# W2 of a macaron block halved to f16 and turned by DMA before its last butterfly

## The reference

```
x = x + 0.5 * ffn(layernorm(x), W1, W2, W3)
x = x + attn(layernorm(x), qkv_w, qkv_norm_w, proj_w, proj_norm_w, norm_w, s)
x = x + 0.5 * ffn(layernorm(x), W1, W2, W3)

ffn(x):  hidden = fwht(silu(x @ W1.T) * (x @ W3.T))      # H = 2048, Hadamard transform over H, / sqrt(H)
         return hidden @ W2.T
attn:    q, k, v = rmsnorm(x) @ ternary(qkv_w).T          # weights rounded to -1, 0, 1 times a scale
         16 heads of 32, decaying linear attention in chunks of 128, two rmsnorms, @ ternary(proj_w).T
```

## Time and profile before

| | us |
|---|---|
| median of 3 runs (lowest, highest) | 2405.73 (2405.51, 2408.26) |
| profiled execution: own time | 2411.79 |
| profiled execution: span | 2410.1 |
| TensorE busy | 2366.8 |
| VectorE busy | 1173.1 |
| ScalarE busy | 719.5 |
| GpSimd busy | 162.8 |
| first stage ends | 111.1 |
| second stage ends | 207.6 |
| W2 stage ends | 232.2 |
| first down stage ends | 278.0 |

### The profile page before, as it was taken

The page is one execution under the profiler, slowest core; times in us unless marked ns, Lnnn a source line. Parts: engine busy times, 40 slices in busy tenths (PEclk is TensorE's granted clock), DMA queues, the critical chain, the costliest instruction groups (busy, mean ns, idle before and its releaser), DMA issues.

```text
span 2410.1 us, 32239 instructions
## 1 busy us (share of the span) xinstructions
PE 2366.8 (98%) x13040; PEld 1143.9 (47%) x13040; DVE 1173.1 (49%) x2091; ACT 719.5 (30%) x1205; POOL 162.8 (7%) x111
## 2 busy tenths in 40 slices
PE   7998999999999999999999999999999999999999
PEld 3444445544454455445544554455445544544444
DVE  6566535454455534554455355534564445445312
ACT  6635323222232222232323232232233222222211
POOL 0192000000000000000000000000000000000000
PEclk9999999999999999999999999999999999999999
DMA  7933422042213311222133122301331223020210
GB/s 196 220 134 97 126 88 57 23 133 51 75 40 105 75 45 58 83 66 82 34 114 66 40 79 70 109 27 40 105 75 58 62 53 92 23 79 18 70 35 18
DMA packets 240067, 182.20 MB, mean 76 GB/s; under 512 B 172208, under 2 KB 196784, under 8 KB 236080
## 3 DMA queue, kind: packets, MB, share of 16 engines
q1 hardware_dynamic: 239632, 179.63, 26.9%
q10 hardware_dynamic: 288, 0.52, 0.1%
HBM read 84.68 MB, written 54.53 MB: 58 GB/s over the span
## 4 chain that ended last, share of the span: by engine, by line
PE 91%; DVE 4%; DMA 2%; issue 1%; ACT 1%; SPq 1%; POOL 0%; DVEq 0%; ACTq 0%; POOLq 0%
PE d_bank L1378 26%; PE l_bank L1358 25%; PE g_bank L1358 25%; PE a_bank L1416 5%; PE a_bank L1403 2%; PE a_bank L1482 2%; PE a_bank L1470 2%; PE a_bank L1434 1%; PE a_bank L1464 1%; DVE work L1096 1%; PE a_bank L1448 1%; DVE work L1076 0%; DMA w1t<-q_parts 0%; PE a_bank L1424 0%; DMA parts_dram<-q_parts 0%
## 5 line engine op out<-in xcount | busy, mean ns | idle before, releaser
L1378 PE MATMUL d_bank<-w2t,work 128*128 128x512 f16 x2940 | 674.5, 380 | 0.0
L1076 DVE SCALAR_TENSOR_TENSOR work<-l_bank,l_scale,work 128x512 f32<-128x512 f32 x256 | 191.8, 749 | 548.9 <-PE l_bank L1358 548.8
L1378 PEld LDWEIGHTS d_bank<-w2t,work 128*128 128x128 f16 x2940 | 284.8, 98 | 331.5 <-issue 1.6
L1358 PE MATMUL g_bank<-xt,w1t 128*128 128x512 f16 x1536 | 354.1, 380 | 4.2 <-issue 1.5
L1358 PE MATMUL l_bank<-xt,w3t 128*128 128x512 f16 x1536 | 352.4, 379 | 2.1 <-DVE work L1076 1.3
L815 ACT ACTIVATE work<-g_bank,g_scale 128x512 f32<-128x512 f32 x256 | 175.4, 685 | 575.7 <-PE g_bank L1358 570.0
L1358 PE MATMUL l_bank<-work,w3t 128*128 128x512 f16 x1344 | 308.3, 379 | 0.2 <-DVE work L1076 0.2
L1358 PE MATMUL g_bank<-work,w1t 128*128 128x512 f16 x1344 | 308.3, 379 | 0.0
L834 ACT CAST work<-work 128x512 f16<-128x512 f32 x232 | 143.3, 618 | 520.1 <-DVE work L1076 518.6
L1358 PEld LDWEIGHTS g_bank<-xt,w1t 128*128 128x128 f16 x1536 | 147.7, 98 | 180.4 <-issue 4.8
L1358 PEld LDWEIGHTS l_bank<-xt,w3t 128*128 128x128 f16 x1536 | 147.7, 98 | 171.9 <-issue 1.5
(11 more groups left out here) (198 smaller groups left out, 1749.6 us busy)
## 6 DMA issues: line engine op xcount, KB each, us to landing
work<-parts_dram SPq DMA_DIRECT2D x192, 128.0 KB, 2.7
x_dram<-work SPq DMA_DIRECT2D x16, 1024.0 KB, 3.9
work<-x_dram SPq DMA_DIRECT2D x11, 1024.0 KB, 6.8
parts_dram<-q_parts SPq DMA_DIRECT2D x32, 256.0 KB, 2.0
parts_dram<-k_parts SPq DMA_DIRECT2D x32, 256.0 KB, 2.0
norm_dram<-cent SPq DMA_DIRECT2D x32, 256.0 KB, 2.0
w2t<-in_L_ffn_W_dram SPq DMA_DIRECT2D x30, 256.0 KB, 3.3
xin<-in_L_attn_x_dram SPq DMA_DIRECT2D x7, 1024.0 KB, 8.1
```

What stands on the lines that cost most here:

```text
L1076: nc.vector.scalar_tensor_tensor(out=hfull, in0=l_bank[:], scalar=l_scale[:, j:j + 1], in1=gate, op0=ALU.mult, op1=ALU.mult).then_inc(hful ...
L1358: ins = nc.tensor.matmul(dst[:], wt[:, wp, k, P * j:P * (j + 1)], src[:, xp, k, :], start=(k == 0 and wp == xp), stop=(k == KT - 1 and wp ...
L1378: ins = nc.tensor.matmul(d_bank[t][:], parts[:, hp, P * t:P * (t + 1)], w2t[:, wp, j, :], start=(j == 0 and hp == wp), stop=(j == HT - 1 a ...
```

## The change

Six edits, all in the preparation:

- The Hadamard product takes over one more of the 11 stages: GpSimd does three stages a quarter of W2 (BUTTERFLIES 4 to 3), and w2pair makes the last one by adding and subtracting the products of block i and block i + 8, with a positive and a negated f16 Hadamard matrix.
- W2 is split into two f16 parts in its own layout (w2split, 16 chunks of 128x512, ScalarE and VectorE, 4 buffers) and each chunk's pair of parts is turned by a DMA transpose from SyncE into w2t. w2turn and the fp32 w2had go. w2pair reads w2t, multiplies in f16 into two alternating pairs of banks, and ScalarE and VectorE write the results back over w2t.
- All of W2 is loaded at row blocks 12 to 15 of the first stage; the squares, butterflies, wtop, wfit and splits all lie in the second stage. The first butterfly writes into xt (w2f[0]) and so waits for the last lin of the first stage.
- The norm of batch 2 moves from the second stage to the first down stage (slots 0 to 5). The load of x for it follows the sums of the qkv_w quarters, whose buffer moved to the memory of the mask.
- The signs are turned by 16 DMA transposes from a ring of four buffers; qturn goes from TensorE and ScalarE. SyncE sends the first one after down 7.
- The reload of the qkv and proj rows (wst) is issued right behind the last W2 split.

```diff
-    BUTTERFLIES = HT.bit_length() - 1
+    BUTTERFLIES = HT.bit_length() - 2
+    CHUNKS = 4
+    TERNS = 4
...
+        qst = x_next
+        w2f = [xt_whole[:]] + [w2n[:, t, :] for t in range(KT - 1)]
...
-        had_bank = [g_bank, l_bank]
-        a_bank16 = [b[:].bitcast(F16).rearrange("p (a k t) -> p a k t", a=2, k=KT) for b in a_bank]
+        pair_bank = [a_bank, [g_bank, l_bank]]
...
-                if j >= HT - 2:
-                    steps += [("w2sum", j - (HT - 2)), flies[j - (HT - 2)]]
-            steps += [("begin", 1), ("next_x", 2)]
+            steps += [("begin", 1), ("next_q", 0)]
             own = {}
-            for q in range(2, 2 * KT):
-                add(own, (4, 4, 9, 9, 16, 16)[q - 2] + q % 2, [("w2sum", q)])
-            for i, fly in enumerate(flies[2:]):
+            for q in range(2 * KT):
+                add(own, q, [("w2sum", q)])
+            for i, fly in enumerate(flies):
                 add(own, 2 * i, [fly])
-            for q in range(2 * FOURTHS):
-                add(own, 3 + 2 * q, [("qsum", (q // 2, q % 2))])
-            for i, part in enumerate(norm_steps(("ffn1", 2))):
-                add(own, 18 + 2 * i, part)
-            add(own, 29, [("wtop", 0)])
-            add(own, 31, [("wfit", 0), ("qmean", 0)])
+            add(own, 9, [("wtop", 0)])
+            add(own, 12, [("wfit", 0)])
+            splits = (13, 14, 16, 18) + tuple(range(19, 31))
+            for i, at in enumerate(splits):
+                add(own, at, [("w2split", i)])
+            for q, at in enumerate((2, 4, 6, 8, 10, 11, 15, 17)):
+                add(own, at, [("qsum", (q // 2, q % 2))])
+            add(own, 21, [("qmean", 0), ("next_x", 2)])
...
+            steps += [("w2pair", i) for i in range(HT // 2)]
+            own = {}
+            for i, part in enumerate(norm_steps(("ffn1", 2))):
+                add(own, i, part)
+            add(own, 6, [("decay", 0)])
+            for i in range(8):
+                add(own, 5 + i, [("qscale", i)])
+                add(own, 7 + i, [("qprep", 2 * i), ("qprep", 2 * i + 1)])
+            add(own, 12, [("fit", 0)])
...
-                    if m and c in (12, 13):
-                        load_w2(0, c % 2)
+                    if m and c >= 12:
+                        load_w2(c - 12, 0)
+                        load_w2(c - 12, 1)
...
+                elif step == "w2split":
+                    t, q = divmod(arg, CHUNKS)
+                    sp.wait_ge(w2_lo, arg + 1)
+                    sp.dma_start_transpose(w2t[:, CHUNKS * q:CHUNKS * (q + 1), :, P * t:P * (t + 1)].rearrange("p j a d -> p (j a) d"),
+                                           w2_parts[arg % 4].rearrange("p j a d -> p (j a d)")).then_inc(w2_turned[arg % 4], 16)
+                    if arg == KT * CHUNKS - 1:
+                        for w in range(FOURTHS):
+                            sp.dma_start(wst[:, 4 * w:4 * w + 4, :], quarter(w)).then_inc(wst_loaded[w], 16)
+                elif step == "qprep":
+                    r = arg
+                    sp.wait_ge(q_tern, r + 1)
+                    if r == 0:
+                        sp.wait_ge(d_step, 8)
+                    dst, col = (wqkv, r) if r < QKV_T else (wproj, r - QKV_T)
+                    sp.dma_start_transpose(dst[:, :, P * col:P * (col + 1)], tern[:, r % TERNS, :]).then_inc(q_turned[r % TERNS], 16)
...
-                    src, dst = (w2n[:, t, :], w2p) if st % 2 == 0 else (w2p, w2n[:, t, :])
+                    src, dst = (w2n[:, t, :], w2f[t]) if st % 2 == 0 else (w2f[t], w2n[:, t, :])
...
+                            pool.wait_ge(l_ready, HT)
...
+                elif step == "w2split":
+                    t, q = divmod(arg, CHUNKS)
+                    act.wait_ge(w2_but, t + 1)
+                    act.wait_ge(w2_f, 1)
+                    if arg < 2:
+                        act.wait_ge(w_turned[2 + arg], 16 * 2 * HT // 4)
+                    elif arg < 4:
+                        act.wait_ge(flipped[arg - 2], flips(("ffn1", 1), arg))
                     else:
+                        act.wait_ge(w2_turned[arg % 4], 16 * (arg // 4))
+                    nc.scalar.activation(w2_parts[arg % 4][:, :, 0, :], w2f[t][:, D * q:D * (q + 1)].rearrange("p (j d) -> p j d", d=P), ACT.Copy,
+                                         scale=w2_scale[:]).then_inc(w2_hi, 1)
+                elif step == "w2pair":
+                    act.wait_ge(w2_had, arg + 1)
+                    for half, j in enumerate((arg, arg + HT // 2)):
+                        nc.scalar.activation(w2t[:, j, 0, :], pair_bank[arg % 2][half][:], ACT.Copy, scale=f2[:, j:j + 1]
+                                             ).then_inc(w2_final_hi, 1)
...
+                    nc.vector.tensor_scalar(w2_scale[:], tiny[:, 5:6], PRE_SCALE, None, ALU.mult)
                     link(power(tiny[:, 4:5], top_all[:, 0:1], True))
+                    nc.vector.tensor_scalar(f2[:], f2[:], tiny[:, 4:5], 2.0 / 2.0 ** 6 * W_SCALE * 0.25 / PRE_SCALE,
+                                            ALU.mult, ALU.mult).then_inc(w2_f, 1)
...
+                elif step == "w2split":
+                    t, q = divmod(arg, CHUNKS)
+                    dve.wait_ge(w2_hi, arg + 1)
+                    parts = w2_parts[arg % 4]
+                    nc.vector.scalar_tensor_tensor(out=parts[:, :, 1, :], in0=w2f[t][:, D * q:D * (q + 1)].rearrange("p (j d) -> p j d", d=P),
+                                                   scalar=w2_scale[:], in1=parts[:, :, 0, :], op0=ALU.mult,
+                                                   op1=ALU.subtract).then_inc(w2_lo, 1)
+                elif step == "w2pair":
+                    for half, j in enumerate((arg, arg + HT // 2)):
+                        dve.wait_ge(w2_final_hi, 2 * arg + half + 1)
+                        nc.vector.scalar_tensor_tensor(out=w2t[:, j, 1, :], in0=pair_bank[arg % 2][half][:], scalar=f2[:, j:j + 1],
+                                                       in1=w2t[:, j, 0, :], op0=ALU.mult, op1=ALU.subtract).then_inc(w2_final_lo, 1)
...
+                    r = arg
+                    if r == 0:
+                        for t in (2, 3):
+                            dve.wait_ge(flipped[t % 2], flips(("ffn1", 2), t))
+                    elif r >= TERNS:
+                        dve.wait_ge(q_turned[r % TERNS], 16 * (r // TERNS))
+                    dve.wait_ge(q_scaled, r + 1)
+                    signs, negative = tern[:, r % TERNS, :], tern[:, TERNS + r % 2, :]
+                    link(nc.vector.tensor_scalar(negative, wst[:, r, :], -0.5, None, ALU.is_lt))
+                    nc.vector.scalar_tensor_tensor(out=signs, in0=wst[:, r, :], scalar=0.5, in1=negative, op0=ALU.is_gt,
+                                                   op1=ALU.subtract).then_inc(q_tern, 1)
...
+                elif step == "w2pair":
+                    i, banks = arg, pair_bank[arg % 2]
+                    if i == 0:
+                        pe.wait_ge(dve_const, 2)
+                        for b in range(4):
+                            pe.wait_ge(w2_turned[b], 16 * KT * CHUNKS // 4)
+                    elif i == 1:
+                        pe.wait_ge(gate_ready, 2 * HT)
+                        pe.wait_ge(hfull_ready, 2 * HT)
                     else:
+                        pe.wait_ge(w2_final_lo, 2 * (i - 1))
+                    for second in range(2):
+                        for j, sign in ((i, 0), (i + HT // 2, second)):
+                            for part in range(2):
+                                ins = nc.tensor.matmul(banks[second][:], hadamard[:, sign, :], w2t[:, j, part, :],
+                                                       start=(j == i and part == 0), stop=(j > i and part == 1))
+                    ins.then_inc(w2_had, 1)
```

More of the change, by code:

```diff
@@ L22 @@
 W_SCALE = 2.0 ** 15
+PRE_SCALE = 2.0 ** 14
 QKV_SCALE = 2.0 ** 6
@@ L59, in macaron_kernel @@
         w3t = sb("w3t", [P, 2, KT, H], F16)
-        w2t = sb("w2t", [P, 2, HT, D], F16)
+        w2t = sb("w2t", [P, HT, 2, D], F16)
         wqkv = sb("wqkv", [P, KT, 3 * D], F16)
@@ L368, in first_steps @@
-            own = {1: [("decay", 0)], 4: [("qscale", 0)], 5: [("qprep", 0), ("qscale", 1)]}
-            for r in range(8):
-                own[6 + r] = [("qturn", r)]
-                if r < 6:
-                    own[6 + r] = [("qscale", r + 2)] + own[6 + r]
-                if r < 7:
-                    own[6 + r] += [("qprep", r + 1)]
-            add(own, 9, [("fit", 0)])
+            steps += [("w2pair", i) for i in range(HT // 2)]
+            own = {}
+            for i, part in enumerate(norm_steps(("ffn1", 2))):
+                add(own, i, part)
@@ L531, in _ @@
                     sp.dma_start(hid_dram[arg], spill[arg % 2]).then_inc(hid_stored[arg % 2], 16)
-                elif step == "w2had" and arg == HT - 1:
-                    for j in (HT - 2, HT - 1):
-                        b, fill = filled("w2turn", j)
```

(35 more changed lines are left out.)

92 lines of the change are left out of this document (21 added, 71 removed).

## The result

The changed kernel is slower: 2416.28 us as the median of 6 runs (2412.47 to 2417.35) against 2406.15 of the kernel before on the same chip (2405.09 to 2408.26), a ratio of 1.0038 with a 95% interval of 1.0026 to 1.0049. The forecast was 2399.7, with a range of 2390 to 2412. The profiled execution after took 2415.66 us, its span is 2413.7.

A forecast was written before the change was run, and what follows sets the result against it. TensorE, busy 98% of the span, was taken as the bound, with only the first 278 us edited. Terms +2.3 - 1.7 - 4.5 - 2.1 = -6.0 us took 2405.7 to 2399.7 us, range 2390 to 2412.

The forecast's parts named there:

- Second stage: Gate and lin of the second feed-forward: fewer butterflies, added splits, 94.8 against 96.5 us, -1.7 (-8 to +7).
- The holds: Second stage: GpSimd's butterflies hold VectorE's splits and low halves, two or three a pair; TensorE stands 9.9 us with wfit.
- First stage: First feed-forward's gate and lin: W2 loads ahead of transposes make the last three gates late, +2.3 us (0 to +6).
- the loads pile up: First stage: three more megabytes push the transposes by 6 instead of 2.3 us, with a restart; +5, 2404.7 us; chance 0.09.
- W2 stage: f16 products replace fp32 transposes and products; with a 3.0 us transpose wait and 1 restart, 20.1 against 24.6: -4.5 us.
- First down stage: Sign transposes leave TensorE, but the residual and next down stage come 1 to 3 us late: -2.1 us (-4.4 to +2).
- The rival of SyncE's ring: First down stage: sign transposes cost 2 us of SyncE's queue each, stage ends 14 us late, 2411.7 us; chance 0.12.
- Sum: Whole kernel: the four stage terms, +2.3 - 1.7 - 4.5 - 2.1, make -6.0 us.
- a sign of being wrong that the prediction had named: Behind the prologue: the prediction is wrong if that unedited part moves by itself.
- The forecast of -6: Whole kernel: -6.0 us from the runs' median of 2405.7, to 2399.7 us.

The follow-up runs named there:

- best_top_elem: best with the maximum reduction behind wtop replaced by an elementwise addition (computes something else): 2396.97 us, ratio 0.9957 to the kernel before.
- top_elem: Changed kernel with the maximum reduction behind wtop (slot 9) replaced by an elementwise addition, the mean's reduction kept at slot 21: 2402.82 us, ratio 0.9983 to before.
- qmean_last: Changed kernel with the reduction for the mean moved from slot 21 to slot 31, behind the last butterfly: 2406.17 us, ratio 0.9996 to before.
- fit_last: Changed kernel with the fit of the scale moved from slot 12 to 15 of the first down stage, behind the last sign row: 2418.64 us.
- reduce_pool_only: Changed kernel with GpSimd's sum for the mean still at slot 21 and only VectorE's part moved to slot 31: 2414.34 us, ratio 1.0035 to before.
- best: Changed kernel with mean at slot 31, W2 loads spread later, five reloads earlier, fit later, last split at slot 29: 2396.43 us, ratio 0.9960 to before.

## Why the prediction was wrong

- **Second stage, the step that failed.** "With two reductions the last butterfly ends some 67 us in" put the switches of GpSimd at nearly nothing, and the two moves (wtop to slot 9, the mean to slot 21) at "lin 6 is ready 0.5 us late". Measured, each reduction among butterflies costs GpSimd 12.8 or 13.7 us, the last butterfly ends 91.6 us in, and lin 12 waits 14.69 us with a restart of 2.5 behind it. Without a reduction among the butterflies the last one ends 66.3 us in (best_top_elem), so the butterflies were sized rightly and the switches were what the sum put at nothing; no rival had them either. The term of -1.7 came out as +7.0. The runs put the difference on this: without the first switch 13.5 us less, with the mean behind the butterflies 10.1 less. I had followed the waits behind wfit and not the one behind the mean: VectorE's queue holds a low half, a split and the evacuation of lin 11 behind it, and TensorE's lin 12 needs that one.
- **The holds.** They came, but fewer: held splits took 2.2 to 2.8 us and held low halves 1.1 to 2.8, at most two to a pair where two or three were forecast. TensorE's lin 11 waits 2.7 us (3.5 forecast), its lin 8 not at all (4.8 forecast), since GpSimd stood in its gap there; in top_elem, which has no such gap, lin 8 waits 4.1. In qmean_last the stage's waits sum to 6.6 us against 9.9 in the prediction.
- **First stage.** The mechanism was right, the size low: +5.0 (the range had 0 to +6) against +2.3. In this execution a restart (4.45 for 12 products instead of 2.76) came on top of the late transposes; but in top_elem and qmean_last, whose first stage is the same, there was no restart and it was still +4.2 and +4.3, so the transposes themselves came later than forecast. The rival "the loads pile up" comes 5 us on top of the forecast, a first stage of +7.3; what was measured lies about halfway between the two.
- **W2 stage.** -5.7 against -4.5. The wait for the last transpose was 2.93 us (3.0 forecast), the pairs 2.06 us apart as worked out (2.1); the restart of 1 us did not come, 1.89 us for the first eight products (it came in five of the other kernels, 2.90 to 3.29 us).
- **First down stage.** -1.2 against -2.1 and a restart of 1.5 us into the next stage that the sum did not have. The last sign row was done 43.8 us in (41.6 to 43.5 forecast). The rival of SyncE's ring had its condition fulfilled: it decides from 1.3 us a row, and 1.58 was measured. The excess of 0.28 us over 16 rows is 4.5 us at most, and 3.0 of wait came of it, not 12.
- **Sum.** +5.0 + 7.0 - 5.7 - 1.2 + 1.5 = +6.6, and 6.67 is what the trace shows; the medians say 10.1. The own times of the two profiles differ by 3.9: the stall in before's execution, 2.7 us and a slow group of 12 behind it (4.34 instead of 2.75), takes 4.3 off 6.67, and the wait of 1.44 us at 2028.83 puts 1.4 on. That wait comes with the change: all eleven kernels that have the change show it, with 0.97 to 1.52 us, and neither of the two without it does, so the part after the prologue moved by itself, a sign of being wrong that the prediction had named. By the traces the change costs 6.67 + 1.4, some 8.1 us, and the medians say 10.1; the last 2 us lie within the spread of the executions (2405.09 to 2408.26 and 2412.47 to 2417.35) and stay open. In the runs the change of the median follows that of the q_parts group within 1.1 us (-10.1 for -9.6, -4.3 for -5.2, -13.5 for -14.5, -19.9 for -19.6), except in fit_last and reduce_pool_only, which are off by 1.7 and 2.7; of these, 1.7 and 0.9 lie in a first stage that ended later in those executions (117.82 and 117.00 against 116.12).
- **The sign.** The six edits as such can be faster than before: best, which keeps them and changes only the order of steps and loads (partly back to the one of before, partly to a new one), is 10 us faster. The forecast of -6 was for the order as it stood, and that one is slower.

What stays open is what GpSimd does in the gaps. That they come with a change between elementwise work and a reduction over the partitions, in both directions, and not between two reductions, is shown by the rows above; that it is a load of code is only what the passage of the Trainium skill suggests, and no run tested it.

## What to carry to other kernels

An instruction's duration is not its price: for each kind of work that is moved between others on an engine, look in the trace for what the engine did just before and after it, also for gaps that end with "issue", and keep steps of the rare kind side by side. Then follow the queue of each engine that waits for it: a 0.4 us reduction cost TensorE 14.7 us because VectorE, in its written order, had the next evacuation behind the wait. A gap on an engine is worth what stands behind it, 13.5 us in one order and nothing in another, so an order is repaired by moving the waiter to where the engine is ahead.

## What the runs showed of the hardware

- GpSimd: 5.5 to 5.9 us ahead of a reduction over the partitions that follows elementwise work, 6.6 to 8.3 us behind it (10.0 once, in top_elem), none between two reductions (one case, in the kernel before).
- TensorE after the wait of 14.69 us, as the stretches of that time show (length, busy time, granted clock behind the counts): the clock had fallen to 0.50, its level of 1.2 GHz, while it stood, and stayed there through the next 13 matmuls, after which it was back at 2.4.

```profile
195.90:198.60 2.70, 0.00 (x0) 0.00 (x0) 2.52 (x8) 0.00 (x0) 0.05 (x1) 0.50 0.18 71
198.60:204.00 5.40, 5.37 (x13) 1.94 (x14) 2.05 (x4) 2.42 (x4) 0.96 (x1) 0.50 0.73 166
204.00:219.00 15.00, 15.00 (x70) 6.80 (x69) 9.56 (x12) 7.61 (x12) 3.69 (x2) 0.99 0.59 127
```

- A wait of 2.3 to 3.0 us had a restart in one place (4.45 for 12 products) and none in another (2.76 behind 2.73), so it was no fixed surcharge. Where a restart came, the granted clock had fallen: 0.50 from 283.1 to 285.0 us, behind the wait of 3.02; from 222.7 to 224.0, behind the wait of 2.93 and without a restart, it was 1.00.
